# Attention units by block of queries, with a plain fp32 P V in two column tiles and the projection moved into the units

## What is computed

```python
# x: (1, 2048, 256), ctx: (1, 1601, 192); 4 heads of 64
xn, ln = layernorm(ctx), layernorm(layernorm_plain(x))
q = ln @ Wq.T
k, v = split(concat([xn @ Wkv.T, ln @ Wlkv.T]))      # 1601 + 2048 keys
attn = softmax(mask(rmsnorm(q) * scale @ rmsnorm(k).T))
x = x + (attn @ v) @ Wo.T + bo
# experts: 8 of them, 2 for a token
xl = layernorm_plain(x)
w, idx = top_k(softmax(xl @ router.T), 2); w = w / (sum(w) + 1e-6)
y = (silu(xl @ gate[e]) * (xl @ up[e])) @ w2[e]      # for each e in idx
x = x + sum(w * y)
```

## Time and profile before

| | |
|---|---|
| three runs, median | 1198.23 us (1196.29 to 1199.64) |
| profiled execution: span from its first to its last instruction | 1197.7 us |
| PE busy | 1054.0 us, 88% |
| DVE busy | 774.5 us, 65% |
| ACT busy | 656.9 us, 55% |
| POOL busy | 518.0 us, 43% |
| moved by DMA | 100.41 MB, mean 84 GB/s |
| mean granted TensorE clock | 0.946 |

### The profile page before, as it was taken

The page is one execution under the profiler, slowest core; times in us unless marked ns, Lnnn a source line. Parts: engine busy times, 40 slices in busy tenths (PEclk is TensorE's granted clock), DMA queues, the critical chain, the costliest instruction groups (busy, mean ns, idle before and its releaser), DMA issues.

```text
span 1197.7 us, 19749 instructions
## 1 busy us (share of the span) xinstructions
PE 1054.0 (88%) x4904; PEld 761.3 (64%) x4905; DVE 774.5 (65%) x1474; ACT 656.9 (55%) x867; POOL 518.0 (43%) x525
## 2 busy tenths in 40 slices
PE   3688689999999999999999999999866268999994
PEld 2455457667666666766666766666555257888884
DVE  4999777766766866766766676686554813444442
ACT  1455446777777777777677677777522012333321
POOL 4012125454544654644645554465410014555553
PEclk9899879999999999999999999999977569999998
DMA  5222402112131111231211211111266777333332
GB/s 162 62 71 71 172 16 69 53 40 70 53 113 58 60 46 53 66 114 45 71 48 48 70 53 49 57 58 47 67 184 209 265 248 199 52 49 52 53 53 26
DMA packets 84392, 100.41 MB, mean 84 GB/s; under 512 B 11035, under 2 KB 78044, under 8 KB 83836
## 3 DMA queue, kind: packets, MB, share of 16 engines
q1 hardware_dynamic: 73694, 89.20, 22.8%
q0 software_dynamic: 7488, 10.23, 5.3%
q10 hardware_dynamic: 3166, 0.46, 0.3%
HBM read 57.60 MB, written 42.26 MB: 83 GB/s over the span
## 4 chain that ended last, share of the span: by engine, by line
PE 70%; DVE 10%; ACT 7%; DMA 5%; issue 5%; SPq 1%; ACTq 1%; DVEq 0%; POOL 0%; POOLq 0%
PE bM L1177 9%; PE bPV L1241 8%; PE bPV L1239 8%; PE bPV L1249 8%; PE bS L1221 7%; PE bS L1222 7%; ACT PT L642 4%; DVE mpart L867 3%; DMA xin<-x 3%; PE bA L1129 2%; PE bG L1340 2%; PE bH L1357 1%; ACT Ph L648 1%; PE bY L1340 1%; PE bY L1342 1%
## 5 line engine op out<-in xcount | busy, mean ns | idle before, releaser
L482 POOL TENSOR_TENSOR Pl<-PT,Ph 128x1024 fp32r<-128x1024 f32 x96 | 230.8, 2404 | 348.5 <-ACT Ph L648 348.5
L867 DVE TENSOR_REDUCE mpart<-bM 128x1 f32<-128x464 f32 x524 | 310.9, 635 | 87.2 <-PE bM L1177 85.9
L642 ACT ACTIVATE PT<-bS 128x1024 f32<-128x1024 f32 (+1 forms) x240 | 239.4, 998 | 139.3 <-PE bS L1222 139.3
L648 ACT CAST Ph<-PT 128x1024 fp32r<-128x1024 f32 (+1 forms) x240 | 245.5, 1023 | 7.0
L894 DVE TENSOR_TENSOR Pl<-PT,Ph 128x1024 fp32r<-128x1024 f32 x144 | 176.1, 1223 | 104.6 <-ACT Ph L648 104.4
L1221 PE MATMUL bS<-Q,S 128*128 128x512 f32 x464 | 185.9, 401 | 1.4 <-ACT Q L633 0.7
L1239 PE MATMUL bPV<-Ph,V 128*65 128x512 f32 x464 | 184.5, 398 | 0.0
L1222 PE MATMUL bS<-Q,S 128*128 128x512 f32 x464 | 184.0, 396 | 0.0
L1241 PE MATMUL bPV<-Ph,V 128*64 128x512 f32 x464 | 183.1, 395 | 0.0
L1177 PE MATMUL bM<-S,Q 128*128 128x464 f32 (+1 forms) x524 | 165.5, 390 | 10.9 <-DVE mpart L867 8.7
L1249 PE MATMUL bPV<-Pl,V 128*65 128x512 f32 x464 | 146.9, 395 | 0.8
(11 more groups left out here) (210 smaller groups left out, 1537.4 us busy)
## 6 DMA issues: line engine op xcount, KB each, us to landing
W<-wsp_d SPq DMA_DIRECT2D x32, 768.0 KB, 5.8
wraw<-w SPq DMA_DIRECT2D x96, 128.0 KB, 2.2
wsp_d<-whi SPq DMA_DIRECT2D x96, 128.0 KB, 1.7
wsp_d<-wraw SPq DMA_DIRECT2D x96, 128.0 KB, 1.7
v_d<-Vs SPq DMA_DIRECT2D x29, 258.0 KB, 3.3
V<-v_d SPq DMA_DIRECT2D x4, 1870.5 KB, 7.6
xall<-x SPq DMA_DIRECT2D x1, 2048.0 KB, 13.6
xin<-x SPq DMA_DIRECT2D x16, 128.0 KB, 3.8
```

The lines of the kernel that those rows point to most:

```text
L482: pool.tensor_tensor(Pl[:, p % 3, :, :], PT[:, p % 3, :, :], Ph[:, p % 3, :, :].bitcast(F32), ALU.subtract)\
L642: act.activation(PT[:, p % 3, 0:w, :], bS[sl][:, 0:w, :], ACT.Exp).then_inc(sem("exp"), 1)
L648: act.copy(Ph[:, p % 3, 0:w, :], PT[:, p % 3, 0:w, :]).then_inc(sem("p_hi"), 1)
L867: dve.tensor_reduce(mpart[:, i, g:g + 1], banks[k % len(banks)][:, 0:PIECE], AX, ALU.max)\
```

## The change

Beside `Fori` loops written out, it does this:

- The 16 units go block by block of queries, four heads in each, so that a block's output is complete after four units.
- P V is plain fp32: no high and low parts of P or V. For each pair of key tiles two matmuls of 64 weight columns are issued, one whose result lies in partitions 0 to 63 of the bank and one in 64 to 127. These are the two column tiles of the title, one for each key tile of the pair. The row sums are made apart: POOL adds up 11 of the 15 steps of P, DVE the others, and `o_T` adds the halves by matmuls (`twin`, `onec`). `outputs` comes three pairs behind the scores, with four buffers of P.
- V stays on chip, and Q is transposed in the prologue.
- Bias, projection, norm and router logits of a token tile go into a unit of the following block (12 tiles); the last four follow the units.
- Of the expert weights, experts 4 to 7 are split in the prologue, in 24 chunks of 512 columns, and the units wait for their stores. Experts 0 to 3 are loaded raw after the units and split in place, by ACT and POOL, in 12 steps of 1024 columns.

```diff
-                    for b, c in tiles:
-                        pe.matmul(bPV[0:D + 1, 0, :], V[:, h % 2, c, 0:D + 1], Ph[:, sl, b, :],
-                                  start=c == 0, stop=False, skip_group_check=True)
-                        pe.matmul(bPV[0:D, 0, :], V[:, h % 2, c, D + 1:VW], Ph[:, sl, b, :],
-                                  start=False, stop=False, skip_group_check=True)
...
-                        last = pe.matmul(bPV[0:D + 1, 0, :], V[:, h % 2, c, 0:D + 1],
-                                         Pl[:, sl, b, :],
-                                         start=False, stop=c == NK - 1, skip_group_check=True)
+                        after(pe, sem("o_cp"), u)
+                    pe.wait_ge(sem("exp"), NP * u + p + 1)
+                    for b, c in enumerate(range(2 * p, min(2 * p + 2, NK))):
+                        last = pe.matmul(bPV[b * D:(b + 1) * D, 0, :], V[:, c, h * D:(h + 1) * D],
+                                         PT[:, p % NPT, b, :], start=c < 2, stop=c >= NK - 2, skip_group_check=True)
                     last.then_inc(sem("pv"), 1)
...
                 for p in range(NP):
                     scores(p)
+                    if p == OUT_AT and not w.first:
                         o_T(u)
-                    if p >= 2:
-                        outputs(p - 2)
+                    if p == HEADS_AT and h % 2 == 0 and not w.first:
+                        pe.wait_ge(sem("o_ev"), u)
+                        heads_T()
+                    if p == Y_AT and w.fin:
+                        pe.wait_ge(sem("o_ev"), u)
+                        pe.wait_ge(sem("oT"), w.pairs)
+                        project(t, bT[:, 0, 0:DIM])
+                    if p == X3T_AT and w.fin:
+                        x3_T(t, bT[:, 0, DIM:2 * DIM], x3[:])
+                    if p == LG_AT and w.fin:
+                        route(t, bT[:, 0, 0:E], x3T)
+                    pieces(p, 0)
+                    if p >= LAG:
+                        outputs(p - LAG)
+                    pieces(p, 1)
...
+            def o_T(n):
+
+                pe.wait_ge(sem("o_cp"), n)
+                pe.wait_ge(sem("zs"), n)
                 for i in range(QB):
+                    at = i * (D + 1)
+                    pe.matmul(bT[:, 0, at:at + D], oT_a[:, i * P:(i + 1) * P], twin[:], start=True, stop=True)
+                    last = pe.matmul(bT[:, 0, at + D:at + D + 1], acc_d[:, 0, i * P:(i + 1) * P], onec[:],
+                                     start=True, stop=True)
...
+            dve.wait_ge(sem("wsplit"), (E - EARLY) * NCH)
+            for j in range(2):
+                dve.wait_ge(sem(f"wst{j}"), (E - EARLY) * NCH // 2 * 32)
+            link(dve.memset(Q2[D:P, :, :].bitcast(F32), 0.0))
...
+            for n in range(NSPL):
+                sp.wait_ge(sem("wsplit"), n + 1)
+                e, c = n // NCH, n % NCH * WC
+                sp.dma_start(wsp_d[e, 0, :, c:c + WC], whi[:, n % 2, :].bitcast(F32)).then_inc(sem(f"wst{n % 2}"), 16)
+                sp.dma_start(wsp_d[e, 1, :, c:c + WC], wraw[:, n % 2, :]).then_inc(sem(f"wst{n % 2}"), 16)
+                sp.wait_ge(sem(f"wst{n % 2}"), 32 * (n // 2) + 32)
+                if n + 2 < NSPL:
+                    load(n + 2)
...
+PIECES = ((0, 1), (2, 0)) + ((2, 1),) * 3 + ((1, 1), (2, 1), (1, 1), (2, 1)) + ((1, 1),) * 5 + ((0, 0),)
+OUT_AT, HEADS_AT, Y_AT, SD_AT, X3T_AT, LG_AT = 5, 7, 8, 9, 11, 12
+XB_AT = 2
+LAG = 3
+POOL_SUMS = ((0, 1),) + tuple((-1, p) for p in range(2, 12))
+DVE_SUMS = ((12, 13), (-1, 14))
```

More of the change, by code:

```diff
@@ L87, in run_steps, with __init__, run_units, after @@
         body(Step(i, lo + 1))
+class Unit:
+    def __init__(self, b, h):
+        self.b, self.h = b, h
+        self.u = H * b + h
+        self.first = self.u == 0
+        self.last = self.u == UNITS - 1
+        self.fin = b > 0
+        self.tile = QB * (b - 1) + h
+        self.pairs = self.u // 2
+        self.next_h = (h + 1) % H
+        self.next_b = b + (h + 1) // H
+def run_units(body):
+    for b in range(NB):
+        for h in range(H):
+            body(Unit(b, h))
+def after(eng, s, n):
+    if n:
+        eng.wait_ge(s, n)
 def build(nc, x, ctx_in, mask, ln_x_g, ln_x_b, ln_l_g, ln_l_b, qn_g, kn_g, w_lat, w_ctx, wo_t, bo,
@@ new lines, in unit @@
+            def unit(w):
+                u, v, t = w.u, w.u + 1, w.tile
+                k = 0
+                for p in range(NP):
+                    if p == OUT_AT and not w.first:
+                        o_out(u, (w.h - 1) % H, w.pairs)
+                    if p == Y_AT and w.fin:
+                        stats2(t, x2[:], bT[:, 0, 0:DIM], st2[:], mv2[:])
+                    if p == SD_AT + 1 and w.fin:
+                        after(dve, sem("ol"), 16 * t)
+                        after(dve, sem("x3T_mm"), t)
+                        norm(t, x2[:], x3[:], mv2[:], sd2[:], rs2[:])
+                    if p == LG_AT + 1 and w.fin:
+                        dve.wait_ge(sem("lg_mm"), t + 1)
+                        dve.tensor_copy(lg[:, t, :], bT[:, 0, 0:E]).then_inc(sem("lg"), 1)
+                    if not w.last:
+                        for _ in range(sum(PIECES[p])):
+                            piece(v, k, M_BANKS)
+                            k += 1
+                        if p == 1:
+                            q_lo(v, w.next_h, w.next_b)
+                if not w.last:
+                    maxima(v)
+                for n in range(ND):
+                    z_sum(w, n)
@@ L970, in _ @@
-            for lo, hi, a in ((2, 3, (1, 0, 0)), (3, 5, (1, 1, 0))):
-                run_steps(dve, lo, hi, lambda s, a=a: fin(s, *a))
+            run_units(unit)
+            o_out(UNITS, H - 1, None)
+            NF = NT - QB
             dve.wait_ge(sem("iota"), 3)
@@ new lines, in unit @@
+                    if p == X3T_AT and w.fin:
+                        x3_T(t, bT[:, 0, DIM:2 * DIM], x3[:])
[5 more added lines that the diff above has]
+                    pieces(p, 1)
+                if not w.last:
+                    if w.fin:
+                        pe.wait_ge(sem("lg"), t + 1)
+                    elif not w.first:
+                        pe.wait_ge(sem("o_ev"), u)
+                        if h % 2 == 0:
+                            pe.wait_ge(sem("oT"), w.pairs)
+                    c_T(v)
```

858 lines of the change are left out of this document (389 added, 469 removed).

## The result

The change made the kernel 0.6% faster: 1192.26 us, the median of five runs (1191.43 to 1193.66), against 1199.64 us for the kernel before in runs beside it (1196.29 to 1201.59). The ratio is 0.9941, 95% interval 0.9926 to 0.9956. The forecast was 1181 us. The span of the profiled run is 1189.5 us, 8.2 us under that of before. The stages of the changed kernel are the answer to the earlier trace rows: the last wait of the prologue and the first maxima, the units, `fin`, routing up to the first gather, and the experts.

A forecast was written before the change was run, and what follows sets the result against it. PE was taken to bound the units. Units +4, start +28, `fin` -48, routing and experts 0 sum to -16: from 1197.7 to 1181 us, own range 1165 to 1200, over all cases 1092 to 1258.

The forecast's parts named there:

- three records a pair: In the units, the two 64-column matmuls of a key-tile pair partly overlap on PE: 1.29 us, 18.1 us a unit.
- no price for the change of width: In the units, the forecast's sum held no cost for PE going between 128-column matmuls and 64-column outputs.
- rival C: In the units, a pair's two tiles overlap fully, two records a pair: -83 us, 1098 us; chance 0.20.
- rival B: In the units, a pair's two tiles do not overlap, four records a pair: +110 us, 1290 us; chance 0.12.
- Rival A: In the units, PE pays 0.166 us at each change between full and half width: 69 us, 1250 us; chance 0.19.
- The start, +28 us: Before the units, waiting for 24 split chunks at 3.9 us each delays the first score: +28 us (+13 to +44).
- Rival D: In the prologue, chunks take 2.3 us or less, so weights do not delay the units: 1141 us; chance 0.11.
- `fin`, -48: After the units, only four of sixteen token tiles remain: 21.5 us against 69.7, so -48 us.
- Routing, at nothing: After the units, POOL's 29 us of splits for experts 0 to 3 lie under DVE's routing chain, adding nothing.
- Experts, 228: The expert stage stays at 228 us, with no change; another length would show the forecast wrong.
- the period of 43 to 45 us: Sign for the forecast: one unit of the changed kernel should last 43 to 45 us.
- DVE ends most waits of PE: Sign against the forecast: DVE or POOL ending most waits of PE in the middle of a unit.

The follow-up runs named there:

- after: The profiled run of the changed kernel itself, no further edit; the changed kernel's median is 1192.26 us, its profiled span 1189.5 us.
- e1_one_tile: Changed kernel with both output matmuls of a pair writing the same column tile from a unit's second pair on: 1362.3 us, ratio 1.136 to the kernel before.
- e12_sp_loads: Changed kernel with the eight raw weight loads after the units issued by SP, behind its loads of x, not by ACT: 1190.9 us.

## Why the prediction was right or wrong

The sign was right, the size was less than half of what was forecast (-7.4 for -17 to -19 us, by either median of before), and the mechanism was wrong where it matters. Three steps failed: the splits of POOL under the routing chain at nothing (22 us lost), three records a pair with no price for the change of width (together with the rest of the unit 26 us too long), and the start (13 us too short). That the total came within 11 us is luck, since these errors cancel.

- *P V at three records a pair*: wrong. It is two, as rival C had it. Its objection, that the written order forbids it, does not hold: the starts are 0, 0, t, t. From this alone the units would have been 83 us shorter than forecast. It also rules out rival B, four records a pair.
- *No price for the change of width*: wrong. Rival A's price was 0.33 us a group, taken from the way out of the array in the earlier trace rows; measured are 0.31. It applies to 12 groups and about once more at the unit's end. The argument for it, that nothing in the trace shows a change of width to be free, overlooked the outputs of the kernel before, which go from 128 to 65 and 64 columns and back at no cost, though in fp32r. A and C came true together, which no case of mine allowed for: 0.86 + 0.31 = 1.17 us a lone pair, by chance near the 1.29 of the forecast. The rest of the unit was priced from above: `o_T` took 1.7 us (511.39 to 513.09) for 2.5, the wait at the start 0.7 for 1.2, the five at the end 2.7 for 2.6. A plain unit is 41.0 us and not 42.85, the stage -22 and not +4.
- *The start, +28 us*: right in mechanism, short by 13. The first split began at 78.0 and not at 73, since the prologue did not speed up as forecast, and a chunk took 4.3 us and not 3.9; the last store landed at 180.65, inside the range of 152 to 183 (whose lower bound of 3.3 us a chunk should be 3.4 by its own terms). Rival D, chunks of 2.3 us, is out with it. Without the split and its wait the kernel is 42 us shorter.
- *`fin`, -48*: right, -46.5, though 3.4 us of what remains are ACT's issuing of the raw loads, which the sum did not hold.
- *Routing, at nothing*: wrong by 22 us, and the step that failed was "lie under the routing chain of DVE". The cover was there in time, but the work under it stops the engine above it. No rival questioned it.
- *DVE beside POOL in the prologue*: not foreseen either, 5.0 us, here hidden by the wait for the stores.
- *Experts, 228*: 225.7; the 2.6 us were not followed up.

Among the signs that I named, the period of 43 to 45 us would have been right only for units with a tile (42.7 to 43.4). "DVE ends most waits of PE" is what the profile says of the weight loads and also of the matmuls in the units, but those are 16.9 us in all, and the run with half reductions shows how little it is worth.

## What to carry to other kernels

Price work that is to be hidden by what it shares with its cover, and not only by whether it fits in time: here POOL's subtractions under a chain of small DVE operations cost a whole POOL instruction for each of twelve of them. Count the changes into column tiles and back beside the matmuls in them, and put more outputs behind each change, but then deal out the work of the slower engine to match the longer and shorter slots. A total that comes out nearly right can be several errors that cancel, so compare stage by stage.

## What the runs showed of the hardware

- Two plain fp32 matmuls of 64 weight columns in different column tiles run side by side in both records: 0.86 us for the pair, 1.72 in one tile (runs `after` and `e1_one_tile`), though the program writes one matmul wholly ahead of the other.
- Going from 128-column matmuls to plain fp32 ones of 64 columns and back costs 0.31 us in all, the same for a group of four records and of eight, and nothing if the plain fp32 matmuls have 128 columns. The fp32r outputs of 64 and 65 columns of the kernel before stand among 128-column matmuls at the usual 0.23 us and pay nothing.
- A DVE operation with two inputs in SBUF, and the small `tensor_scalar` and copy there, waits for one whole POOL instruction: 2.0 to 2.3 us beside subtractions of 2.34, 0.4 to 0.8 beside 0.74. POOL waits for DVE in the same way: 1.17 to 1.97 us for its 0.74 beside longer operations of two inputs. Reductions, and an operation that reads PSUM (0.29 us for `tot<-bR`), do not wait.
- Of eight loads of 0.5 to 1 MB issued in a row by one engine, the seventh took 3.4 to 4.0 us to issue and held up what stood behind it, on ACT and on SP alike; the others took 0.4 to 0.9 us.
- Behind the first maxima, in which PE is busy for 16.4 of 22.8 us, PE enters the units at the lower level of its clock (1.2 GHz): scores follow each other after 0.43 us, later after 0.23 (2.4 GHz). How long this lasts differs from run to run: the granted clock of the first 15.6 us was 0.87 in the changed kernel and 0.69 in `e12_sp_loads`, whose first unit took 1.6 us longer.
